# A two-layer sandwich on one core: blocks of 32x32 and TensorE in place of transposing transfers

## The chip, the cores and the metric

The kernel runs on one core of one Trainium2 chip. The metric is the device time of one execution in microseconds (us), here the median of three runs. One further execution was recorded by the hardware profiler, and every row below is of that one.

The names of the engines are those of the profile: PE is TensorE (PEld its weight loads), DVE is VectorE, ACT is ScalarE, POOL is GpSimd, and SP is SyncE, which here does nothing but wait on semaphores and issue transfers.

## The reference

The input is 4096 tokens of width 512. An attention layer with 16 heads works on 64 fixed latent keys instead of on other tokens, and a ternary feed-forward layer follows. Each is wrapped in a layernorm before and one behind:

```python
Q, V = ln(x) @ Wq.T + bq, ln(x) @ Wv.T + bv
logits = einsum('bhtd,lhd->bhtl', Q, latent) / sqrt(HD)
topk_logits, idx = top_k(logits, 4)              # 4 of the 64 latents
weighted = softmax(topk_logits) @ latent[idx]
x1 = x + ln((weighted + V) @ Wo.T + bo)
wu, wg, wd = (clip(round(w / mean(|w|)), -1, 1) * mean(|w|) for w in (W_up, W_gate, W_down))
hidden = silu(ln(x1) @ wu.T) * (ln(x1) @ wg.T)   # 2048 wide
out = x1 + ln(hidden @ wd.T)
```

## The kernel before, in words

The tokens go through in eight chunks of 512, each of four tiles of 128 tokens. The instruction streams of the five engines are written out by hand and are tied together by semaphores; nothing reorders them. A loop body carries the attention of chunk i together with the feed-forward network (FFN) of chunk i-1. The body `first` has the attention of chunk 0 and all the preparation of the weights, `mid` is a hardware loop over chunks 1 to 6, `last` has the attention of chunk 7, and `tail` only the FFN of chunk 7.

**Precision.** Each f32 operand is split into two fp16 halves, high and low. The high half is a rounded copy on ACT, the low half a subtraction on POOL or DVE. A projection is then three products (hi·hi, hi·lo, lo·hi) on PE.

**Layouts.** PE contracts over partitions, so the normalised rows X of a tile, the top-4 probabilities P and the normalised rows X1 ahead of the FFN must all be turned from token-major to feature-major. Before, SP issues a DMA_TRANSPOSE for each tile: `pt` (L363, P into PT), `transpose_rows` (L313, X into XT and X1 into X1T). Weights arrive as they are and are turned on PE (L449 in f32; L472 in fp16 for the ternary weights).

**One period of the loop.** PE does the FFN's `upgate(e)` for e = 0 to 15 into the four banks `ug` (L562), with the logits (L507) in between, then the value projections v(0) to v(3) (L480), `weigh` (L532, which needs PT of all four tiles), the output projection wo (L545), the down products `down(t)` (L574) between them, and the query projections of the next chunk. Behind the upgates ACT takes tanh, DVE multiplies (L1228, L1233), ACT makes the high half (L818) and POOL the low half `hidden_lo` (L985). The attention of tile t runs beside it: eight maxima for each head on DVE (L1243), the replacing of the top four (L1265), `shift` on POOL (L972), the exponential on ACT, `normalise` on POOL (L979), and `probs_lo` on DVE (L1285).

## Time and profile before

| what | value |
|---|---|
| median of three runs | 1121.09 us (1120.2 to 1122.27) |
| profiled execution, its own time | 1121.47 us |
| its span in the trace | 1119.5 us |
| mean granted clock of PE over the span | 0.955 |
| PE busy | 995.2 us, 89% |
| DVE / POOL / ACT busy | 68% / 48% / 46% |

The span runs from the first to the last instruction that the profiler recorded. The execution's own time is 2.0 us longer. The shares are averages over the whole span, and the first 194 us look very different from the rest; the rows below are picked by stage for that reason.

### The profile page before, as it was taken

The page shows a single profiled execution, that of the slowest core. Times are in us where ns is not written, and L with a number is a line of the kernel's source. Part 1 is how long each engine was busy: PE and PEld are TensorE (multiplying, and loading weights), DVE is VectorE, ACT ScalarE, POOL GpSimd, SP SyncE. Part 2 cuts the span into 40 slices and gives each one's busy share as a digit, 9 for nine tenths or more (in the row PEclk, how much of TensorE's full clock was granted, in tenths as well). Part 3 has the DMA queues.
Part 4 walks back from the last instruction along what each step waited for, and adds up shares of the span by engine and source line. Part 5 has one row for each costly group of instructions (what it writes and reads, how often), then busy time and mean ns, then how long its engine had stood idle before and what let it go on. Part 6 is the DMA issues. An engine that isn't in the chain of part 4 may idle for free.

```text
span 1119.5 us, 18366 instructions
## 1 busy us (share of the span) xinstructions
PE 995.2 (89%) x5876; PEld 492.6 (44%) x5876; DVE 757.5 (68%) x2698; ACT 514.1 (46%) x793; POOL 539.8 (48%) x436
## 2 busy tenths in 40 slices
PE   2533368999999999999999999999999999988997
PEld 1232234544454445444544445444544454434443
DVE  6389666796669846993689477966698469835432
ACT  3368554453455345444455444534553454422331
POOL 1145423365546554665456554655456545632332
PEclk9865599999999999999999999999999999999999
DMA  7921243022421243124402431224212421212001
GB/s 225 357 93 40 39 85 72 24 39 57 95 76 19 50 100 95 19 38 94 104 10 38 94 74 58 38 56 94 76 19 41 109 48 20 39 38 57 1 1 38
DMA packets 152451, 74.65 MB, mean 67 GB/s; under 512 B 136768, under 2 KB 136768, under 8 KB 151360
## 3 DMA queue, kind: packets, MB, share of 16 engines
q1 hardware_dynamic: 152384, 73.95, 26.9%
q8 instruction: 19, 0.31, 0.1%
q14 instruction: 48, 0.39, 0.1%
HBM read 31.99 MB, written 8.39 MB: 36 GB/s over the span
## 4 chain that ended last, share of the span: by engine, by line
PE 58%; DVE 17%; issue 10%; ACT 6%; POOL 5%; DMA 3%; SPq 1%; POOLq 0%; DVEq 0%; ACTq 0%
PE ug L562 35%; PE ug L574 11%; PE ring L480 6%; PE ring L545 3%; PE ring L507 2%; DVE Lr L1265 1%; DMA X1T<-halves 1%; POOL halves L1008 1%; DVE stx L1356 1%; DVE x L1353 1%; DVE halves L1285 1%; DVE row L1333 1%; POOL qaT_lo L966 1%; DVE halves L1223 1%; DVE sty L1336 1%
## 5 line engine op out<-in xcount | busy, mean ns | idle before, releaser
L562 PE MATMUL ug<-X1T,TU 128*128 128x512 f16 (+1 forms) x1152 | 247.3, 358 | 11.9 <-DMA X1T<-halves 6.2
L985 POOL TENSOR_TENSOR hT<-ugt,hT 128x512 f16<-128x512 f32 x128 | 168.9, 1320 | 162.0 <-ACT hT L818 162.0
L562 PE MATMUL ug<-X1T,TG 128*128 128x512 f16 (+1 forms) x1152 | 246.4, 357 | 0.0
L574 PE MATMUL ug<-TD,hT 128*128 128x512 f16 x1024 | 225.0, 379 | 0.0
L811 ACT ACTIVATE ugt<-ug,cu 128x512 f32<-128x512 f32 x128 | 88.0, 687 | 237.1 <-PE ug L562 236.1
L562 PEld LDWEIGHTS ug<-X1T,TU 128*128 128x128 f16 x1152 | 111.5, 99 | 121.8 <-issue 7.2
L1228 DVE SCALAR_TENSOR_TENSOR ugt<-ugt,ug 128x512 f32<-128x512 f32 x128 | 87.4, 683 | 112.8 <-ACT ugt L811 111.3
L562 PEld LDWEIGHTS ug<-X1T,TG 128*128 128x128 f16 x1152 | 113.5, 99 | 109.5
L574 PEld LDWEIGHTS ug<-TD,hT 128*128 128x128 f16 x1024 | 99.8, 98 | 122.7 <-issue 3.9
L1265 DVE MATCH_REPLACE8 Lr<-v,Lb 128x68 f32<-128x68 f32 x512 | 102.3, 211 | 0.0
L1292 DVE BATCH_NORM_STATS2 stf<-ug 128x6 f32<-128x512 f32 x32 | 22.2, 693 | 111.9 <-PE ug L574 111.9
L1233 DVE SCALAR_TENSOR_TENSOR ugt<-ugt,ug 128x512 f32<-128x512 f32 x128 | 87.9, 687 | 4.4
L480 PE MATMUL ring<-XT,wq_hi 128*128 128x512 f16 x256 | 78.0, 387 | 12.9 <-DMA XT<-PT 12.9
L972 POOL TENSOR_TENSOR Lb<-Lb,v 128x1024 f32<-128x1024 f32 x32 | 63.5, 1983 | 53.3 <-DVE Lr L1265 46.4
L979 POOL TENSOR_TENSOR p<-Lb,r 128x1024 f32<-128x1024 f32 x32 | 63.8, 1995 | 48.6 <-issue 38.4
L818 ACT ACTIVATE hT<-ugt 128x512 f16<-128x512 f32 x128 | 79.5, 621 | 2.6 <-DVE ugt L1233 2.6
L480 PE MATMUL ring<-XT,wv_hi 128*128 128x512 f16 x256 | 78.3, 388 | 0.0
L1243 DVE MAX8 v<-Lb 128x8 f32<-128x64 f32 x512 | 69.0, 208 | 7.6 <-ACT Lb L766 7.6
L786 ACT ACTIVATE halves<-p 128x1024 f16<-128x1024 f32 x32 | 33.5, 1047 | 52.0 <-POOL p L979 42.6
L1285 DVE SCALAR_TENSOR_TENSOR halves<-p,halves 128x1024 f16<-128x1024 f32 x32 | 52.8, 1651 | 0.0
L680 ACT ACTIVATE xn<-x,nbx,rsx 128x512 f32<-128x512 f32 x28 | 22.7, 811 | 63.6 <-DVE nbx L1367 43.7
L545 PE MATMUL ring<-wo_hi,qaT_hi 128*128 128x512 f16 x128 | 48.5, 379 | 2.6 <-POOL qaT_lo L966 2.6
(172 smaller groups left out, 1490.6 us busy)
## 6 DMA issues: line engine op xcount, KB each, us to landing
x_in<-in_L_attn_hidden_states SPq DMA_DIRECT2D x8, 1024.0 KB, 5.7
out_dram<-Lr SPq DMA_DIRECT2D x32, 256.0 KB, 3.2
x<-in_L_attn_hidden_states SPq DMA_DIRECT2D x28, 256.0 KB, 3.3
hT<-in_L_ffn_W_up SPq DMA_DIRECT2D x8, 512.0 KB, 7.7
hT<-in_L_ffn_W_down SPq DMA_DIRECT2D x8, 512.0 KB, 4.2
TD<-in_L_ffn_W_gate SPq DMA_DIRECT2D x4, 512.0 KB, 11.7
TU<-in_L_attn_Wq SPq DMA_DIRECT2D x1, 1024.0 KB, 7.8
TG<-in_L_attn_Wv SPq DMA_DIRECT2D x1, 1024.0 KB, 9.4
```

What stands on the lines that cost most here:

```text
L480: last = pe.matmul(ring[:, bank, :], wT[w][a][:, k, m * P:(m + 1) * P], XT[:, b, k, :], start=(n == 1), stop=(stop and n == 3 * KD), skip_ ...
L545: last = pe.matmul(ring[:, bank, :], qaT[a][:, k, t * P:(t + 1) * P], wT[2][b][:, k, :], start=(n == 1), stop=(n == 3 * KD))
L562: last = pe.matmul(ug[:, 2 * (e % 2) + s, cols], w[:, k, e * P:(e + 1) * P], X1T[:, b, k, cols], start=(k == 0 and b == 0), stop=(k == KD ...
L574: last = pe.matmul(ug[:, t, :], hT[:, a, e, t * P:(t + 1) * P], td[:, e, :], start=(e == 0 and a == 0), stop=(e == NE - 1 and a == 1))
L811: act.activation(ugt[:, e % 2, :], ug[:, 2 * (e % 2), :], ACT.Tanh, scale=cu[:, 0:1]).then_inc(tanh_ready, 1)
L818: act.activation(hT[:, 0, e, :], ugt[:, 2 + e % 2, :], ACT.Copy).then_inc(h_hi, 1)
L985: pool.tensor_tensor(hT[:, 1, e, :], ugt[:, 2 + e % 2, :], hT[:, 0, e, :], ALU.subtract).then_inc(h_lo, 1)
L1228: dve.scalar_tensor_tensor(out=ugt[:, e % 2, :], in0=ugt[:, e % 2, :], scalar=1.0, in1=ug[:, 2 * (e % 2), :], op0=ALU.add, op1=ALU.mult).t ...
L1233: dve.scalar_tensor_tensor(out=ugt[:, 2 + e % 2, :], in0=ugt[:, e % 2, :], scalar=HS, in1=ug[:, 2 * (e % 2) + 1, :], op0=ALU.mult, op1=ALU ...
L1243: last = dve.max(v8[:, t % 2, h, :], Lb[:, t % 2, h, 0:NL])
L1265: last = dve.match_replace(Lr[:, h, :], v8[:, t % 2, h, :], Lb[:, t % 2, h, :], HIT)
L1285: dve.scalar_tensor_tensor(out=halves[:, 1, :], in0=Pb, scalar=PS, in1=halves[:, 0, :], op0=ALU.mult, op1=ALU.subtract).then_inc(p_lo, 1)
```

## The change

It does four things.

1. No transfer transposes. X1 goes through PE: `turn_x1` does eight transposes of each tile into a bank of PSUM, and a copy on ACT (three tiles of a chunk) or DVE (one) brings it to X1T. P and X are turned on DVE in blocks of 32x32, and plain transfers then move the blocks between partitions: 16 for each tile of P (L469), and two times 16 for a chunk's X (L481). PT and XT are laid out in blocks of 32 columns for it.
2. The host lays out Wq, Wv, Wo, the latents and the FFN's weights transposed. PE's transposes of weights and their evictions are gone. A ternary piece is now a rounding in place on DVE (`round_to`, 24 of them) and a sign on ACT.
3. On POOL a `warm` partition_all_reduce on a zeroed tile stands at the very start, all_maxima(0) comes between the low halves of tile 0 and tile 1, and the low halves of P of tiles 0 to 2 are made on POOL (for tile 2 behind `normalise(3)`), with DVE keeping tile 3.
4. A new body `second` is split from the loop for chunk 1. It carries 14 of the roundings beside its FFN, with the signs that follow them and with all_sum(2) on POOL in the middle. The order of PE in the loop becomes v0 v1 down0 v2 v3 down1 weigh down2 wo down3, and in the tail the last statistics close on DVE.

```diff
-            def transpose_rows(dst, t, src, done):
-                sp.dma_start_transpose(dst[:, :, :, t * P:(t + 1) * P].rearrange("p s k t -> p (s k) t"),
...
-                    sp.dma_start_transpose(PT[:, :, :, t * P:(t + 1) * P].rearrange("p s k t -> p (s k) t"),
-                                           halves[:, :, :].rearrange("p s d -> p (s d)")).then_inc(p_t, 16)
+                    src = prob_halves(kind, t).rearrange("p u s d -> p u (s d)")
+                    for a in range(4):
+                        for u in range(4):
+                            sp.dma_start(PT[BLK * u:BLK * u + BLK, 4 * t + a, :, :, :].rearrange("p s j t -> p (s j t)"),
+                                         src[BLK * a:BLK * a + BLK, u, :]).then_inc(p_t[t % 2], 16)
...
+                def turn(bank, half, done):
+                    for b in range(8):
+                        last = pe.transpose(bank[:, b * P:(b + 1) * P], half[:, b * P:(b + 1) * P], id16[:, :])
+                    last.then_inc(done, 1)
...
+            pool.memset(warm[:, :], 0.0).then_inc(consts, 1)
+            pool.partition_all_reduce(warm[:, 1:2], warm[:, 0:1], P, RMAX).then_inc(warmed, 1)
...
+            def round_to(n):
+                w, src = n // NPIECE, (again_d if n >= 2 * NPIECE else stages[n // NPIECE])[n % NPIECE]
+                dve.tensor_scalar(src, src, iw[:, w:w + 1], MAGIC, ALU.mult, ALU.add).then_inc(rounded, 1)
...
+                def turn(t):
+                    wait(dve, p_raw, i, TT, t + 1)
+                    wait(dve, p_lo, i, TT, t)
+                    dve.transpose(turned[:, :, :].rearrange("p u (j l) -> p u j l", l=BLK),
+                                  Pb.rearrange("p (j u l) -> p u j l", u=4, l=BLK)).then_inc(p_turned, 1)
```

**POOL at the start.** In the order of the built programs, POOL began like this before; `rs` is the first layernorm's reciprocal root, `ma` the maxima, `tota` a sum, and `qaT_lo` a low half of Q.

```order
L930 TENSOR_TENSOR rs<-va,nh 128x4 [waits ln1_var,consts]
L940 ISA
L940 ISA ma<-mg 128x2 [waits mg_ready]
L946 ISA tota<-tot 128x1 [waits tot_ready]
L962 ISA
L962 TENSOR_TENSOR qaT_lo<-p,qaT_hi 128x512 [waits q_hi] x3
L940 ISA
L940 ISA ma<-mg 128x2 [waits mg_ready]
L962 ISA
L962 TENSOR_TENSOR qaT_lo<-p,qaT_hi 128x512 [waits q_hi]
```

And now, with the low halves of X in `PT`:

```order
L1305 ISA
L1305 ISA warm<-warm 128x1 [waits consts]
L1309 ISA
L1309 TENSOR_TENSOR rs<-va,nh 128x4 [waits ln1_var]
L1326 TENSOR_TENSOR PT<-qaT_hi,PT 128x512 [waits x_hi]
L1317 ISA
L1317 ISA ma<-mg 128x2 [waits mg_ready]
L1326 ISA
L1326 TENSOR_TENSOR PT<-qaT_hi,PT 128x512 [waits x_hi]
L1326 TENSOR_TENSOR PT<-qaT_lo,PT 128x512 [waits x_hi] x2
L1342 TENSOR_TENSOR qaT_lo<-p,qaT_hi 128x256 [waits x_lo,qa_hi]
```

A reduction with its two reconfigurations now stands ahead of `rs`, and another behind the first low half. Over the whole program there are 12 reconfigurations where there were 8.

**SP in the loop.** SP's rows for the probabilities before, one transfer for a tile, with the REGISTER_ALU rows between them left to the waits:

```order
L229 REGISTER_ALU
L363 DMA_TRANSPOSE PT<-halves 128x16x128 [waits p_lo,vw_done]
L229 REGISTER_ALU
L363 DMA_TRANSPOSE PT<-halves 128x16x128 [waits p_lo,vw_done] x2
L229 ISA
```

And now, for the last two tiles and what stands behind them:

```order
L256 REGISTER_ALU
L469 DMA PT<-halves 32x512 [waits p_lo,vw_done]
L469 DMA PT<-halves 32x512 x15
L469 DMA PT<-halves 32x512 [waits p_lo,vw_done]
L469 DMA PT<-halves 32x512 x15
L256 ISA
L486 ISA [waits out_ready]
```

Each tile's one instruction has become sixteen in SP's queue, 64 for a chunk, and the store of the output and the transfers of X stand behind them.

**POOL at the end of the loop's FFN.** Before, `hT` being the FFN's hidden values and `Lb` and `p` the logits and probabilities:

```order
L972 TENSOR_TENSOR Lb<-Lb,v 128x16x64 [waits replaced]
L229 REGISTER_ALU
L985 TENSOR_TENSOR hT<-ugt,hT 128x512 [waits h_hi]
L229 REGISTER_ALU
L930 TENSOR_TENSOR rs<-va,nh 128x4 [waits ln1_var]
L979 TENSOR_TENSOR p<-Lb,r 128x1024 [waits p_lo,p_raw,recip_ready]
```

And now:

```order
L1372 TENSOR_TENSOR p<-Lb,v 128x1024 [waits p_turned]
L256 REGISTER_ALU
L1383 TENSOR_TENSOR hT<-ugt,hT 128x512 [waits h_hi]
L1377 TENSOR_TENSOR p<-p,r 128x1024 [waits e_ready,recip_ready]
L1357 TENSOR_TENSOR halves<-turned,halves 128x4x256 [waits p_hi]
L256 REGISTER_ALU
L1309 TENSOR_TENSOR rs<-va,nh 128x4 [waits ln1_var]
```

The normalising of tile 3 has moved ahead of the reciprocal root, and the low half of tile 2 (`halves`, L1357) has come in between.

## Rows read from the trace of the kernel before

**Rows 1.** The page: span and busy time of each engine
```profile
span 1119.5 us, 18366 instructions
...
PE 995.2 (89%) x5876; PEld 492.6 (44%) x5876; DVE 757.5 (68%) x2698; ACT 514.1 (46%) x793; POOL 539.8 (48%) x436
```

**Rows 2.** Windows: start:end, length, busy PE, PEld, DVE, ACT, POOL, clock, DMA share, GB/s
```profile
0.00:194.00 194.00, 87.54 (x612) 53.59 (x612) 131.94 (x390) 106.54 (x157) 63.65 (x50) 0.77 0.45 128
194.20:251.50 57.30, 57.24 (x352) 28.53 (x353) 47.53 (x212) 27.97 (x46) 28.52 (x20) 0.96 0.16 42
434.00:553.00 119.00, 119.00 (x707) 57.85 (x706) 86.11 (x324) 56.48 (x89) 66.02 (x54) 1.00 0.27 62
```

**Rows 3.** Timeline of TensorE in a middle period: start, length, instruction
```profile
489.97 0.59 PE L480 MATMUL ring<-XT,wv_hi 128*128 128x512 f16 x2
...
514.24 0.62 PE L532 MATMUL ring<-PT,latV_hi 64*32 64x512 f16 x16
```

**Rows 4.** Chain that ended last, in the first body: start, length, what
```profile
13.22 3.27 issue
...
33.20 1.15 ACT ug L725 x2
...
48.19 7.57 issue
56.20 7.41 issue
...
130.10 5.79 issue
...
191.05 3.08 DMA X1T<-halves
```

**Rows 5.** Timeline of GpSimd in the first body
```profile
9.16 1.03 POOL L930 TENSOR_TENSOR rs<-va,nh 128x4 f32<-128x4 f32 x1 [6.34 <-DVE va L1177]
16.49 0.37 POOL L940 PARTITION_ALL_REDUCE ma<-mg  x1 [6.31 <-issue]
```

**Rows 6.** Groups of VectorE: line, shapes, count, busy us, mean ns, idle before
```profile
L1285 DVE SCALAR_TENSOR_TENSOR halves<-p,halves 128x1024 f16<-128x1024 f32 x32 | 52.8, 1651 | 0.0
...
L1280 DVE SCALAR_TENSOR_TENSOR Lb<-Lr,Lb 128x1024 f32<-128x1024 f32 x32 | 39.3, 1230 | 0.0
...
L1137 DVE TENSOR_SCALAR ugt<-hT,nhw 128x1024 f16<-128x1024 f32 x8 | 6.0, 746 | 0.0
```

**Rows 7.** Timeline of TensorE: eight fp16 transposes and the next product
```profile
142.01 0.62 PE L472 MATMUL ug<-id,ugt 128*128 128x128 f16 x8 [2.50 <-DVE ugt L1144]
142.47 0.59 PE L480 MATMUL ring<-XT,wv_hi 128*128 128x512 f16 x2
```

**Rows 8.** Timeline of GpSimd at the end of a first FFN stage
```profile
496.23 2.14 POOL L985 TENSOR_TENSOR hT<-ugt,hT 128x512 f16<-128x512 f32 x1
...
502.45 1.90 POOL L979 TENSOR_TENSOR p<-Lb,r 128x1024 f32<-128x1024 f32 x1
```

**Rows 9.** Timeline of SyncE's queue: three reloads issued back to back
```profile
142.98 1.39 SPq L398 DMA_DIRECT2D x<-in_L_attn_hidden_states  x3
```

**Rows 10.** Timeline of SyncE in a middle period: one reload alone
```profile
510.83 0.34 SPq L377 DMA_DIRECT2D x<-in_L_attn_hidden_states  x1
```

**Rows 11.** Timeline of SyncE at the start: four loads of 512 KB
```profile
3.55 2.59 SPq L309 DMA_DIRECT2D hT<-in_L_ffn_W_up  x4
```

**Rows 12.** DMA issues: transfers, KB each, median us from issue to landing
```profile
x<-in_L_attn_hidden_states SPq DMA_DIRECT2D x28, 256.0 KB, 3.3
```

**Rows 13.** The chain that ended last, its part in the tail
```profile
967.08 5.18 PE ring L480 x24
...
982.86 4.26 DMA PT<-halves
...
1028.52 5.17 PE ug L562 x32
...
1112.09 0.71 DVE stf L1292
```

More of the change, by code:

```diff
@@ L49 @@
 TINY = 2.0 ** -100
+NPIECE = 8
+MAGIC = 1.5 * 2.0 ** 23
+HT = CH // 2
+BLK = 32
+PMOVES = 16 * 16
+ON_PE = ()
+MOVED = tuple(t for t in range(TT) if t not in ON_PE)
+LATL = KD * 2 * NL
+LATV = H // 2 * HD
+SMALL = LATL + LATV + 2 * KD
 def ring_jobs(kind):
@@ L70, in ring_plan, with build @@
     at = len(before)
-    return {job: (n % 4, seq[n + at - 4] if n + at >= 4 else None) for n, job in enumerate(jobs)}
-def build(nc, x, Wq, bq, Wv, bv, Wo, bo, lat, Wu, Wg, Wd, out):
+    plan = {job: (n % 4, seq[n + at - 4] if n + at >= 4 else None) for n, job in enumerate(jobs)}
+    if kind == "first":
+        for t in range(TT):
+            plan["WO", 0, t] = (2 + t % 2, ("WO", 0, t - 2) if t >= 2 else None)
+    if kind == "second":
+        for job in (("Q", 0, 0), ("T", -1, 0)):
+            plan[job] = (plan[job][0], None)
+    if kind == "last":
+        for t, bank, freed in ((0, 2, ("WO", 0, 2)), (1, 3, ("WO", 0, 3)), (2, 1, ("WO", 0, 1)), (3, 2, ("T", 0, 0))):
+            plan["T", 0, t] = (bank, freed)
+    return plan
+def build(nc, x, Wq, Wv, Wo, small, bo, Wu, Wg, Wd, out):
     NCH = x.shape[0] * x.shape[1] // CH
@@ new lines, in wide, with down_bank, x_bank @@
+        def wide(v, rows):
+            return v.rearrange("p (a l) -> p a l", l=NL) if len(rows.shape) == 3 else v
+        def down_bank(kind, t):
+            if kind == "last" and t == TT - 1:
+                return ring[:, plans["last"]["WO", 0, 0][0], :]
+            return ug[:, t, :]
+        def x_bank(kind, c, t):
+            if kind == "first" and c == 0:
+                bank = ug[:, t, :]
+            elif kind == "first" and t < 2:
+                bank = ring[:, t, :]
+            else:
+                bank = ug[:, t % 2, :]
+            return bank.bitcast(F16)
@@ L412, in body @@
                 if ffn and nxt:
                     reload(2)
+                if ffn:
                     out(2)
[L415 to L420 removed]
                     out(3)
@@ new lines, in body @@
+                    x0_lo(0)
+                    all_maxima(0)
+                    x0_lo(1)
+                    x0_lo(2)
+                    x0_lo(3)
+                    for m in range(KD):
+                        low_q_half(m, 0)
+                    all_maxima(1)
+                    for m in range(KD):
+                        low_q_half(m, 1)
+                    shift(0)
+                    normalise(0)
+                    shift(1)
+                    probs_lo(0)
+                    normalise(1)
@@ new lines, in body @@
+                    probs_lo(1)
+                    shift(2)
+                    all_sum(0)
+                    normalise(2)
+                    for m in range(KD):
+                        low_a_half(m, 0)
+                    shift(3)
+                    probs_lo(2)
+                    ln1_rstd_of(1)
+                    normalise(3)
+                    rstd_y(0)
+                    probs_lo(3)
+                    rstd_y(1)
+                    rstd_x(0, 0)
+                    rstd_x(0, 1)
@@ new lines, in body @@
+                    for m in range(KD):
+                        low_a_half(m, 1)
+                    all_sum(1)
+                    s1_lo(1, 0)
+                    s1_lo(1, 1)
+                    s1_lo(1, 2)
+                    s1_lo(1, 3)
+                    rstd_y(2)
+                    rstd_y(3)
+                    rstd_x(0, 2)
+                    rstd_x(0, 3)
+                    return
+                for m in range(KD if att else 0):
+                    low_q(m)
+                late = kind == "second"
```

1381 lines of the change are left out of this document (894 added, 487 removed).

## The prediction, made blind

> **What bounds the kernel now.** I read the page first: PE is busy 995.2 us of the span of 1119.5 [rows 1]. An average over stages says little, so the windows come next. In a middle period PE works 119.00 of 119.00 us at full clock, while DVE has 86.11 and POOL 66.02 [rows 2]: the loop is bounded by TensorE's own work. The value products v(0) of chunk i start every 119.28 us, from (967.08 - 489.97) / 4 [rows 3, 13], so under 0.4 us of a period is idle. In the first 194 us PE works 87.54 and its mean clock is 0.77 [rows 2]. There nothing is full: DVE 131.94, ACT 106.54, POOL 63.65. What sets that stretch is a chain, and the chain that ended last shows pieces called "issue" of 3.27, 7.57, 7.41 and 5.79 us [rows 4]. On POOL they lie around the partition_all_reduce: the first has 6.31 us idle ahead of it with no releaser, though rs ahead of it ended at 10.19 and the maxima came only at 13.2 (the issue piece starts at 13.22) [rows 4, 5]. I read this as the change of POOL's code, which starts as soon as the instruction before it is done and takes 6 to 7.5 us in each direction, while the reduction itself takes 0.37 [rows 5]. A rule of the Trainium skill stands beside this (GPSIMD Engine Reference, Instruction dispatch): the first call of a freshly loaded kernel pays about 6 us; the trace agrees, and shows that the way back pays it as well.
>
> The changed kernel thus has three places to win or lose: the first body, the body of chunk 1, and the loop, where anything added to PE or waited for by PE is paid in full six times.
>
> **First body: about 14.5 us earlier.** It is a chain through POOL. Warm starts at about 2 us and costs a change each way, 6.3 + 0.4 + 6.8, which ends rs near 18 where it ran at 9.16 [rows 5]. The low half of tile 0 follows at 21, then all_maxima(0) with its two changes, 13.5 us, to 34. Three low halves, the scaled weights and eight half-width query products take 14 us, to 48. all_maxima(1), with the 7.57 and 7.41 of the row and 0.4 between them [rows 4], ends at 63.6, just where it did before. Then ACT has 22 absolute sums; two took 1.15 a piece in the chain with their reading out [rows 4], about 27 us, and with the exponentials between them I take 32, to 96. all_sum(0) on POOL takes 93.4 to 106.4, the attention of tiles 2 and 3 and its low halves reach 136, all_sum(1) with two changes 149.2, the low halves of chunk 1's rows and a pair of copies 164.2, and four query products with the turns of X1 178.7. Before, the same point was at 194.26 less the roughly 1.1 us that the first upgates lost to half clock behind the wait for X1T [rows 4]: 193.2. The gain is 14.5. Of the 48 f32 and 192 fp16 transposes of weights that vanish from PE nothing counts, since PE was busy under half of this stretch [rows 2]. Bounds: with all ten changes hidden (the five pairs are 68.6 us, of which ACT's sums would still keep about 6) it would be 116; with all ten at 7.8, the longest of the chain's pieces and its start [rows 4], it would be 188.
>
> **The body of chunk 1: about 12.7 us later.** From the first upgate to v(0) it took 57.3, with DVE busy 47.53 [rows 2]. DVE now gets 14 roundings at 0.746 [rows 6] = 10.4, three block transposes of 1024 columns, and a copy of X1 of about 1.1; it gives two low halves of 1.65 to POOL [rows 6]. No row has a block transpose: I take 1.23, the row of the 1024-wide f32 select beside it, in bounds of 0.75 and 2.1 (one and near three passes) [rows 6]. That is 47.5 + 10.4 + 3.7 + 1.1 + 0.7 of small ones - 3.3 = 60.1 of work. It had 9.8 us of idle there; I leave it 5.9 of that, so that the stage takes 66. On top, all_sum(2) holds POOL for two changes: the low half of hidden 7 comes some 13 us late, the `ug` banks are not freed, and upgate(11) waits. I take 5.5 of the 7.6 that this comes to, since part coincides with DVE's lag: 71.5, so 58.8 + 12.7. Bounds: 58.8 if all of it fits, 77.8 with no idle saved and the full wait. v(0) of chunk 1 then starts at 178.7 + 71.5 = 250.2, against 251.5 [rows 2].
>
> **The loop: 4.5 us more in each period.**
> - *Transposes on PE.* Eight of them delay the next product by 142.47 - 142.01 = 0.46 us [rows 7]. Four tiles: +1.84, wholly on PE and without cover. The 0.35 of idle may absorb some: I subtract it.
> - *DVE at the head of the loop.* Two rounds of maxima now come ahead of hidden(0), so upgate(2) waits for its bank: +0.9 (bounds 0 and 2.1).
> - *The wait of weigh.* PE needed PT 514.24 - 489.97 = 24.3 us after v(0) [rows 3]. The low half of hidden 15 ended on POOL 8.4 after v(0) because shift(3) stood ahead of it [rows 8]; shift(3) is now earlier, so I put normalise(3) (1.90 [rows 8]) and the low half of tile 2 behind it at 11.1 (bound 9.2). From there SP must issue 32 transfers one behind another. The three reloads of 1.39 give a pitch of (1.39 - 0.43) / 2 = 0.48 [rows 9]; one alone takes 0.34 [rows 10]; at the start it is 2.59 / 4 = 0.65 [rows 11]. Mine have 32 partitions, not 128: I take 0.42. The last lands 2.2 behind its issue, below the 3.3 of 256 KB [rows 12]. So 11.1 + 31 x 0.42 + 2.2 = 26.3, and PE waits 26.3 - 24.3 = 2.0, say 2.1 with the semaphore. Behind weigh stand down(2), wo and the whole second half of the period on PE, so nothing hides it. Ends: 9.2 + 31 x 0.34 + 1.5 = 21.2 gives no wait; 11.1 + 31 x 0.48 + 3.3 = 29.3 gives 5.0; at 0.65 it is 10.
>
> Together 1.84 - 0.35 + 0.9 + 2.1 = 4.5: a period of 123.75. X's 32 transfers land about 48 us behind v(0) and are needed at 52, so they cost nothing while the pitch stays below 0.55. The period from chunk 1 to 2 lacks the first body's idle and comes to 122.3. ACT's three copies of X1 in a period (1.0 us each) lie beside 56 us of work in 119 [rows 2] and are hidden.
>
> A rule of the Trainium skill speaks against this part (DMA: Bandwidth & Descriptors, Rules for kernel authors): many small transfers should be coalesced, since below 64 KB one pays mostly overhead. Each of these has 32 KB. In this trace the share of the DMA engines is only 0.27 [rows 2], so what it would cost here is the queue's pitch, which is the term above.
>
> **The tail.** weigh of the last chunk waited 4.26 for a transposing transfer [rows 13]; that wait becomes one for 16 plain ones, about 1.1 later. The first upgates of the tail are released about 3 us earlier, since a bank no longer waits for the statistics ahead of 1028.52 [rows 13], but PE is behind by the reordering of down(3). The close on DVE instead of POOL saves 1.5 behind 1112.09 [rows 13]. Together 152.0 where it was 152.4.
>
> **Sum.** 250.2 + 122.3 + 5 x 123.75 + 152.0 = 1143.3 of span. Before, the profiled run took 2.0 more than its span and lay 0.4 above the median, so the median comes to 1144.
>
> **The rivals.**
> - *A. As worked out*, 1144, in its own range of 1136 to 1154: chance 0.44.
> - *B. SP's queue is slower than I take it.* The ground for it is the start, where four issues took 2.59 [rows 11]; against it, the 0.48 of rows 9. At 0.6 weigh waits 7.7 instead of 2.1: 5.6 in each of six periods, so 1144 + 34 = 1178; at 0.5 it is 1158. With it goes the dearer block transpose (2.1 instead of 1.23), which makes DVE late for P by 3.5 in a period of which perhaps 1.5 to 1.8 reaches PE: 1144 + 10 = 1154. Chance 0.18, from 1154 up. A page of the Trainium skill (VectorE: DVE Perf Modes, The three transpose paths) gives 311 ns for 128x128 in bf16; by eight times that my 1024 columns would take 2.5 us, and the time would be the 1154 named here. No row here shows one.
> - *C. POOL's changes of code mostly lie under other work* (the other side). The switch ahead of a reduction begins before its data is ready, as it did at 10.19; if the data is always late, only the ways back cost, and warm costs nothing at all. Then the first body ends at about 150 instead of 178.7, chunk 1's v(0) at 221.5, and the time is 1144 - 28.7 = 1115; with PE also free of a wait in the loop (-12.6) 1103, and with no cost of the changes at all 1080. It decides from the point where v(0) of chunk 1 starts before 226: the loop and the tail give back 6 x 4.5 - 2 = 25, which is what the start must win. For it: DVE and ACT had 62 and 87 us of idle in the first 194 [rows 2]. Against: the chain passes through four of the waits already. Chance 0.25.
> - *D. Between them*, 1119 to 1136: SP's pitch is 0.37 and PE never waits for PT (1144 - 12.6 = 1131), or the roundings fit into chunk 1's FFN (1144 - 12.7 = 1131), or both. Chance 0.13, with 0.04 of it within 0.2% (2.2 us) of before, which is what a measurement of this kernel can tell from no change.
>
> The range of 1106 to 1168 leaves out the far ends of B and C, about 0.1 each. Faster 0.25, same 0.05, slower 0.70.
>
> **What would show it.** In the changed trace: rs on POOL at about 18 instead of 9; 11 to 15 us around each reduction; the first upgate of chunk 1's body near 179; v(0) of chunk 1 near 250, and DVE over 90% busy in the 70 us ahead of it; v(0) to v(0) of 123.75 in the loop; PE idle by about 2 us ahead of weigh with a DMA of PT as the releaser; 0.46 us for eight transposes. I am wrong above all if the start of v(0) of chunk 1 lies before 226 or if weigh waits over 5 us.

## The result, and the profile after

The changed kernel takes 1254.9 us (median of four runs, 1252.5 to 1256.0) against 1121.7 of the kernel before, measured beside it: a ratio of 1.118, with an interval of 1.116 to 1.121. It is 133 us slower. The prediction said slower, at 1144, and its range ended at 1168.

The page of the changed kernel, with its span, its busy times and the granted clock in 40 slices, answers to [rows 1]:

```profile
span 1250.6 us, 19370 instructions
...
PE 1023.4 (82%) x6112; PEld 500.5 (40%) x6112; DVE 778.9 (62%) x2740; ACT 551.2 (44%) x843; POOL 553.8 (44%) x469
...
PEclk9966769879889989998999989998999899998999
```

PE has 28 us more of busy time and 131 us more of span: most of the loss is waiting. The windows answer to [rows 2]; they are the first body, the FFN beside chunk 1's attention, the rest of that body up to v(0) of chunk 2, and one period of the loop:

```profile
0.00:192.80 192.80, 73.21 (x584) 43.12 (x585) 92.85 (x341) 98.81 (x157) 60.36 (x63) 0.77 0.28 107
192.80:277.20 84.40, 67.18 (x394) 32.28 (x393) 55.70 (x226) 48.73 (x71) 34.13 (x24) 0.88 0.08 25
277.20:421.30 144.10, 125.28 (x737) 60.18 (x736) 98.91 (x342) 63.77 (x98) 70.15 (x57) 0.93 0.19 53
689.70:823.40 133.70, 123.77 (x738) 59.88 (x736) 92.68 (x335) 59.40 (x91) 68.49 (x56) 0.96 0.17 48
```

The forecast had the first upgate at 178.7 (it came at 192.8), v(0) of chunk 1 at 250.2 (277.2), v(0) of chunk 2 at 372.5 (421.3), periods of 123.75 (133.9 on average) and a tail of 152.0 (1250.6 - 1090.7 = 159.9). The miss of 107.3 us of span is thus 14.1 in the first body, 12.9 in the FFN of chunk 1, 21.8 in the rest of that body, 50.6 in five periods, and 7.9 in the tail. Of the two signs of being wrong that the prediction named, one came true: weigh waits over 5 us.

One point of the kernel before has to be set right. The prediction takes 194.2 for the start of chunk 1's body [rows 2], but TensorE's timeline of the kernel before has the first upgate earlier:

```profile
185.93 1.04 PE L562 MATMUL ug<-X1T,TU 128*128 128x256 f16 x8
...
194.26 1.87 PE L562 MATMUL ug<-X1T,TU 128*128 128x256 f16 x8 [4.67 <-DMA X1T<-halves]
```

At 194.26 it only goes on, behind a wait. So the first body before took 185.9 us and the FFN beside chunk 1's attention 65.7, not 57.3. The first body has become 6.9 us longer, and that FFN 18.7.

**One period of the loop.** SP's timeline of the changed kernel, which answers to [rows 9 to 11]; "x64" rows merge issues whose first starts at the first column and whose last ends that many us later:

```profile
662.66 58.16 SPq L469 DMA_DIRECT2D PT<-halves  x64
...
722.36 10.27 SPq L481 DMA_DIRECT2D XT<-xh  x16
...
738.06 10.20 SPq L481 DMA_DIRECT2D XT<-xh  x16
748.59 0.34 SPq L495 DMA_DIRECT2D x<-in_x  x1
```

GpSimd's timeline at the end of the FFN, for [rows 8]:

```profile
696.45 1.90 POOL L1377 TENSOR_TENSOR p<-p,r 128x1024 f32<-128x1024 f32 x1 [1.07 <-DVE r L1709]
698.30 2.13 POOL L1357 TENSOR_TENSOR halves<-turned,halves 128x1024 f16<-128x1024 f32 x1
```

v(0) of this period began at 689.7. The low half of tile 2 ends at 700.4, 10.7 behind it (11.1 forecast). From there 32 issues fill SP up to 720.8: 0.64 us each, not 0.42. Sixteen issues for X take 10.27, again 0.64. TensorE's timeline shows what waits, for [rows 3, 7]:

```profile
722.19 1.05 PE L723 MATMUL ring<-PT,latV_hi 64*32 64x512 f16 x16 [8.13 <-DMA PT<-halves]
...
724.88 8.13 PE L782 MATMUL ug<-TD,hT 128*128 128x512 f16 x32
...
750.12 0.59 PE L582 MATMUL ring<-XT,wq_hi 128*128 128x512 f16 x2
...
752.71 0.61 PE L589 MATMUL ring<-id,xh 128*128 128x128 f16 x8
...
759.31 0.61 PE L589 MATMUL ring<-id,xh 128*128 128x128 f16 x8 [0.37 <-DVE xh L1654]
...
762.34 1.04 PE L765 MATMUL ug<-X1T,TU 128*128 128x256 f16 x8
```

The same places in the timeline of the kernel before, whose v(0) is at 489.97 [rows 3]:

```profile
515.66 7.08 PE L574 MATMUL ug<-TD,hT 128*128 128x512 f16 x32
...
539.84 0.59 PE L480 MATMUL ring<-XT,wq_hi 128*128 128x512 f16 x2
...
550.20 1.04 PE L562 MATMUL ug<-X1T,TU 128*128 128x256 f16 x8
```

weigh starts 32.5 behind v(0), after 8.13 us of idle that a transfer of PT ended, where it started 24.3 behind [rows 3]. The down product behind it takes 8.13 where it took 7.08; that its time equals the idle's is chance. The four turns of X1 are the L589 rows, of which one waits 0.37 for the last tile. Two windows show the clock behind the wait, and the FFN:

```profile
722.20:732.80 10.60, 10.60 (x80) 4.31 (x81) 0.00 (x0) 5.05 (x8) 4.62 (x4) 0.77 0.32 87
762.30:823.40 61.10, 59.66 (x394) 30.89 (x392) 51.77 (x215) 31.78 (x52) 36.21 (x26) 1.00 0.14 42
```

In the 10.6 us from weigh on the mean granted clock is 0.77: TensorE runs part of them at 1.2 GHz, after 8 us of idle. So the 14.4 us that a period gained split like this: 8.2 up to weigh, 2.3 from weigh to q(0), the first query product (the clock), 1.9 from q(0) to the first upgate (three turns of 0.46 and the wait), and 2.0 in the FFN (the fourth turn and two waits of 0.7). The landing itself is quicker than I took it, as the page's rows of transfers say:

```profile
PT<-halves SPq DMA_DIRECT2D x448, 32.0 KB, 1.8
...
XT<-xh SPq DMA_DIRECT2D x192, 32.0 KB, 1.9
```

**The first body.** GpSimd's timeline, for [rows 5]. The idle in brackets ahead of a reduction is the change of code towards it, that of the row behind it the change back:

```profile
10.45 0.38 POOL L1305 PARTITION_ALL_REDUCE warm<-warm  x1 [8.67 <-issue]
21.33 1.05 POOL L1309 TENSOR_TENSOR rs<-va,nh 128x4 f32<-128x4 f32 x1 [10.50 <-issue]
...
31.17 0.37 POOL L1317 PARTITION_ALL_REDUCE ma<-mg  x1 [5.85 <-issue]
38.56 1.14 POOL L1326 TENSOR_TENSOR PT<-qaT_hi,PT 128x512 f16<-128x512 f32 x1 [7.02 <-issue]
...
61.33 0.37 POOL L1317 PARTITION_ALL_REDUCE ma<-mg  x1 [9.90 <-issue]
73.42 1.29 POOL L1342 TENSOR_TENSOR qaT_lo<-p,qaT_hi 128x256 f16<-128x256 f32 x2 [11.72 <-issue]
...
111.93 0.40 POOL L1321 PARTITION_ALL_REDUCE tota<-tot  x1 [5.80 <-issue]
119.33 1.89 POOL L1377 TENSOR_TENSOR p<-p,r 128x1024 f32<-128x1024 f32 x1 [6.99 <-issue]
```

The changes cost 8.67 and 10.50 us around warm, 5.85 and 7.02 around the first maxima, 9.90 and 11.72 around the second, 5.80 and 6.99 around the first sum. I had 6.3 to 7.6 for all. What differs between them is the traffic, seen in windows over four of these gaps (the last two columns are the share of the DMA engines and GB/s):

```profile
10.90:21.30 10.40, 0.00 (x0) 0.00 (x0) 0.00 (x0) 0.00 (x0) 0.00 (x0) 1.00 0.99 406
25.60:31.20 5.60, 0.88 (x8) 0.61 (x6) 0.00 (x0) 3.43 (x5) 0.03 (x1) 1.00 0.00 0
61.80:73.40 11.60, 0.00 (x0) 0.00 (x0) 1.01 (x8) 0.00 (x0) 0.00 (x0) 0.50 0.77 288
112.40:119.30 6.90, 0.00 (x0) 0.00 (x0) 0.00 (x0) 0.00 (x0) 0.00 (x0) 0.50 0.00 0
```

Where the DMA engines are idle a change costs 5.8 to 7.0; where they are busy, 8.7 to 11.7. The share alone does not give the size. In the kernel before, two changes towards a reduction met busy DMA engines too, in these windows:

```profile
10.20:16.40 6.20, 3.24 (x17) 2.72 (x15) 3.12 (x7) 5.45 (x8) 0.00 (x0) 1.00 0.79 295
48.00:55.70 7.70, 1.76 (x34) 1.50 (x29) 0.00 (x0) 0.00 (x0) 0.00 (x0) 0.50 0.88 348
```

They took 6.31 [rows 5] and 7.80.

### The profile page after: what moved, and what is told of

It reads as the page before. It is cut to its first block, busy times and chain, and to the rows that moved or that the text cites. A ratio compares the mean times of both kernels' runs of the same rounds, so it can differ in the third digit from the quotient of the medians.

```text
span 1250.6 us, 19370 instructions
## 1 busy us (share of the span) xinstructions
PE 1023.4 (82%) x6112; PEld 500.5 (40%) x6112; DVE 778.9 (62%) x2740; ACT 551.2 (44%) x843; POOL 553.8 (44%) x469
## 4 chain that ended last, share of the span: by engine, by line
issue 26%; POOL 20%; SPq 18%; PE 16%; DVE 11%; ACT 6%; DMA 2%; POOLq 0%; DVEq 0%; ACTq 0%
SPq L469 10%; PE ug L765 8%; SPq L481 8%; POOL hT L1383 6%; PE ug L782 4%; POOL p L1377 4%; POOL p L1372 3%; POOL halves L1357 3%; PE ring L582 2%; DMA x<-in_x 1%; PE ring L744 1%; DVE Lr L1696 1%; DVE ugt L1659 1%; DVE v L1674 1%; POOL qaT_lo L1333 1%
## 5 line engine op out<-in xcount | busy, mean ns | idle before, releaser
L765 PE MATMUL ug<-X1T,TU 128*128 128x512 f16 (+1 forms) x1152 | 249.9, 361 | 22.2 <-DVE ugt L1664 20.3
L1383 POOL TENSOR_TENSOR hT<-ugt,hT 128x512 f16<-128x512 f32 x128 | 148.8, 1162 | 211.7 <-ACT hT L1116 204.4
L582 PE MATMUL ring<-XT,wq_hi 128*128 128x512 f16 (+1 forms) x288 | 80.7, 368 | 9.3 <-DMA XT<-xh 7.4
L1740 DVE STREAM_TRANSPOSE turned<-xn 128x512 f32<-128x512 f32 x24 | 17.1, 711 | 113.6 <-ACT xn L882 113.0
L1372 POOL TENSOR_TENSOR p<-Lb,v 128x1024 f32<-128x1024 f32 x30 | 58.9, 1963 | 27.1 <-DVE v L1674 26.5
L582 PE MATMUL ring<-XT,wv_hi 128*128 128x512 f16 x224 | 66.6, 379 | 0.0
L1377 POOL TENSOR_TENSOR p<-p,r 128x1024 f32<-128x1024 f32 x30 | 57.0, 1900 | 19.2 <-DVE r L1709 8.8
L723 PE MATMUL ring<-PT,latV_hi 64*32 64x512 f16 x224 | 15.1, 623 | 60.5 <-DMA PT<-halves 60.5
L1361 POOL TENSOR_TENSOR qaT_lo<-p,qaT_hi 128x512 f16<-128x512 f32 x28 | 32.4, 1156 | 61.8 <-ACT qaT_hi L1091 60.7
L1051 ACT ACTIVATE halves<-turned 128x1024 f16<-128x1024 f32 x28 | 29.5, 1053 | 54.7 <-DVE turned L1730 54.7
## 6 DMA issues: line engine op xcount, KB each, us to landing
hT<-in_Wu SPq DMA_DIRECT2D x4, 512.0 KB, 10.7
```

Source lines behind the costliest of these rows:

```text
L582: last = pe.matmul(bank, wT[w][a][:, k, m * P:(m + 1) * P], XT[:, cols, b, k, :], start=(n == 1), stop=(stop and n == 3 * KD), skip_group_ ...
L765: last = pe.matmul(ug[:, 2 * (e % 2) + s, cols], w[:, k, e * P:(e + 1) * P], X1T[:, b, k, cols], start=(k == 0 and b == 0), stop=(k == KD ...
L1372: pool.tensor_tensor(prob_buf(kind, t), Lb[:, t % 2, :, 0:NL], v8[:, t % 2, :, 0:1].broadcast_to([P, H, NL]), ALU.subtract).then_inc(shift ...
L1377: pool.tensor_tensor(prob_buf(kind, t), prob_buf(kind, t), r4[:, t % 2, :].rearrange("p (h a) -> p h a", a=1).broadcast_to([P, H, NL]), AL ...
L1383: pool.tensor_tensor(hT[:, 1, e, :], ugt[:, 2 + e % 2, :], hT[:, 0, e, :], ALU.subtract).then_inc(h_lo, 1)
```

## The experiments

Where an experiment leaves work out, its expectation says which. Each ratio is to the kernel before, measured beside it, whose medians lay between 1118.0 and 1121.7. A period is the mean distance of v(0) from chunk 3 on; where X's transfers are late, the first one in the loop is 1 to 2 us longer.

### e1: one transfer for a tile

```diff
-PMOVES = 16 * 16
+PMOVES = 16
...
-                            sp.dma_start(PT[BLK * u:BLK * u + BLK, 4 * t + a, :, :, :].rearrange("p s j t -> p (s j t)"),
-                                         src[BLK * a:BLK * a + BLK, u, :]).then_inc(p_t[t % 2], 16)
+                    sp.dma_start(PT[:, 4 * t:4 * t + 4, :, :, :].rearrange("p a s j t -> p a (s j t)"), src).then_inc(p_t[t % 2], 16)
...
+                    sp.dma_start(xt_runs[:, 8 * n:8 * n + 8, :],
+                                 xh[:, :, :].rearrange("p t (u d) -> p (t u) d", u=4)).then_inc(x_landed[n], 16)
```

> The changed kernel, in which each tile of P goes in one transfer of 128 partitions (128 KB) and each pair of tiles of X in one of 256 KB, instead of 16 each. Left out: the exchange between groups of 32 partitions, so every byte of PT and XT is still written, but with rows in the wrong group. Theory 1 (SP's queue): a plain transfer of 32 partitions takes 0.64 us of SP's queue however small it is, 32 of them stand between the low half of tile 2 and weigh (20.4 us), 32 more for X hold the reload of x behind them. Without them the wait of 8.1 us ahead of weigh is gone, PE stays at full clock, XT and the reload land in time, and a period of the loop comes to 123 to 125 instead of 133.7; over seven chunks with the tail about -70 us, so 1175 to 1190. Rival (the transposes on PE, the block transposes on DVE and the later order on POOL carry the loss): the period stays above 129 and the time above 1215.

Measured: 1162.0 (ratio 1.038, 1.035 to 1.041), a period of 121.76. SP's timeline of this kernel:

```profile
546.08 0.49 SPq L476 DMA_DIRECT2D XT<-xh  x1
...
617.98 43.26 SPq L467 DMA_DIRECT2D PT<-halves  x4
```

One issue takes 0.49, and four tiles of P are spread over 43 us because each waits only for its data. PE no longer idles ahead of weigh. The queue's theory holds, and with 93 us it is worth more than the 70 I gave it. The rest of chunk 1's body falls from 144.1 to 126.8 and the tail from 159.9 to 150.2. A period keeps 2.5 over before: 1.84 of turns and about 0.7 of waiting for a bank in the FFN. Those were my first two terms of the loop, 2.4 together.

### e2: pairs of tiles

```diff
+                    if t % 2 == 0:
+                        return
...
+                            sp.dma_start(PT[BLK * u:BLK * u + BLK, 8 * n + a:8 * n + a + 5:4, :, :, :].rearrange("p a s j t -> p a (s j t)"),
+                                         src[BLK * a:BLK * a + BLK, :, u, :]).then_inc(p_t[n], 16)
```

> The changed kernel with two tiles of P in one transfer: 16 transfers of 64 KB for a pair, issued when the second tile of the pair is ready, so 32 for a chunk instead of 64; the result is the full one. Theory 1: if an issue costs 0.6 to 0.65 whatever it carries, the last pair takes 16 x 0.64 = 10 us from the low half of tile 3 (about 13 us behind v(0)), lands near 25.5, and weigh waits 1 us or less: -7 to -9 us in each of seven chunks, with the clock's share -50 to -75, so 1180 to 1205. If the issue's cost grows with the bytes or descriptors (1.2 us for 64 KB), nothing is won: 1250 within 10. The rival of the DVE and PE chain: 1235 or more.

Measured: 1219.0 (1.089, 1.086 to 1.092), a period of 128.5. It is complete, and 36 us faster than the changed kernel, which is less than expected. The issues did not get dearer with twice the bytes:

```profile
668.63 10.24 SPq L471 DMA_DIRECT2D PT<-halves  x16
```

Sixteen of 64 KB take 10.24 us, 0.64 each. But the last pair, which waits for the low half of tile 3, is issued from 15.7 us behind v(0) on and not from the 13 I assumed, and weigh still waits 3.3 us.

### e3 and e4: no warm, and no reduction at all

```diff
-            pool.partition_all_reduce(warm[:, 1:2], warm[:, 0:1], P, RMAX).then_inc(warmed, 1)
```

and for e4 also

```diff
-                pool.partition_all_reduce(tota[:, w:w + 1], tot[:, w:w + 1], P, RADD).then_inc(tota_ready, 1)
+                pool.tensor_tensor(tota[:, w:w + 1], tot[:, w:w + 1], tot[:, w:w + 1], ALU.add).then_inc(tota_ready, 1)
...
```

The maxima are replaced in the same way, and the factor behind the sums is 64 times as large.

> The changed kernel without the reduction on a zeroed tile at the very start. Theory 2 (POOL's changes of code set the first body): rs ran at 21.3 because warm and its two changes of code take it from 1.8 to 21.3; without them rs runs at 9 to 10, and the first body ends 8 to 12 us earlier: -8 to -12 in all. Rival a (ACT and DVE set it from 60 us on): the chain catches up by the waits for all_maxima(1), under 3 us. Rival b (warm does what its name says, the later changes are cheap only because of it): the first change behind it gets dearer by 5 us or more and the time is within 3 us of before or worse.

> The changed kernel without any partition_all_reduce: the two maxima and three sums on POOL are an ordinary addition of the same columns with itself, so that scales are those of a partition and not of the matrix, which is the part left out, and warm is left out too. Every wait stays. Theory 2: the six reductions with twelve changes of code hold POOL 19.5 + 13.2 + 22 + 13.2 + 13.8 us in the first body, and 13 in the next; with all gone the first upgate comes 45 to 60 us earlier than 192.8 (the rest is bounded by ACT's sums), and the FFN of chunk 1 loses 5 to 10 of its 84 us: -50 to -70 in all, 1180 to 1200. Rival (loads, ACT and DVE bound the first body): under -20.

Measured: e3 1244.8 (1.113, 1.109 to 1.116), e4 1188.0 (1.061, 1.058 to 1.065). In e3 the first upgate comes at 181.8 instead of 192.8, so warm's price passes through the whole first body. GpSimd's timeline of e3:

```profile
20.78 0.37 POOL L1316 PARTITION_ALL_REDUCE ma<-mg  x1 [8.10 <-issue]
...
50.43 0.37 POOL L1316 PARTITION_ALL_REDUCE ma<-mg  x1 [9.50 <-issue]
62.84 1.29 POOL L1341 TENSOR_TENSOR qaT_lo<-p,qaT_hi 128x256 f16<-128x256 f32 x2 [12.05 <-issue]
```

The first maxima stand 10.4 us earlier than in the changed kernel. The change towards them is 2.3 us dearer than with warm (8.10 against 5.85, now beside the loads) and not 5 or more, and the time falls by 10, so rival b falls. In e4 the first upgate comes at 134.6, 58 us earlier, and v(0) of chunk 1 at 210.5, 67 earlier: the first body is a chain through POOL's changes of code, as the prediction took it. What a reduction costs is mostly not the reduction (0.4 us).

### e5: sixteen wide transfers

```diff
-                            sp.dma_start(PT[BLK * u:BLK * u + BLK, 4 * t + a, :, :, :].rearrange("p s j t -> p (s j t)"),
-                                         src[BLK * a:BLK * a + BLK, u, :]).then_inc(p_t[t % 2], 16)
+                            sp.dma_start(PT[:, 4 * t + a, :, :, :].rearrange("p s j t -> p (s j t)")[:, P * u:P * u + P],
+                                         src[:, a, P * u:P * u + P]).then_inc(p_t[t % 2], 16)
```

> The changed kernel with 16 transfers for each tile of P as before, but each of 128 partitions by 256 bytes instead of 32 partitions by 1 KB (the same 32 KB). Left out: the exchange between groups of partitions. It tells what the 0.64 us between issues hangs on. If on the number of transfers queued back to back: weigh waits about 8 us as in the changed kernel, time 1250 within 10. If on the partitions or pieces in a transfer: at 0.48 a piece (as one of 128 partitions took alone in the kernel with one move for a tile) the wait falls by 5 and the time to about 1215; if it grows with 128 rows of 256 bytes, it is over 1280.

Measured: 1256.5 (1.122, 1.120 to 1.125), a period of 133.9. SP's timeline, where 64 issues take what they took in the changed kernel (58.16):

```profile
664.58 58.37 SPq L469 DMA_DIRECT2D PT<-halves  x64
```

Neither 128 partitions for 32, nor twice the bytes (e2), changes the pitch: for these transfers from SBUF to SBUF it is paid by the issue. It is not one number for the whole queue. In the changed kernel seven loads of 512 KB were issued back to back between 43.05 and 46.30, one every 0.47 us. What makes the difference was not tried.

### e6: the kernel before without its reductions

```diff
-                pool.partition_all_reduce(ma[:, 2 * g:2 * g + 2], mg[:, 2 * g:2 * g + 2], P, RMAX).then_inc(ma_ready, 1)
+                pool.tensor_tensor(ma[:, 2 * g:2 * g + 2], mg[:, 2 * g:2 * g + 2], mg[:, 2 * g:2 * g + 2], ALU.add).then_inc(ma_ready, 1)
```

The sums are replaced as in e4.

> The kernel before, without its five partition_all_reduces (each an ordinary addition of the same column, so that scales are a partition's own; this is the part left out). Theory 2 says that the start of this kernel too is set by POOL's changes of code: 8 changes, of which 7.2 + 7.6 + 7.4 + 5.8 us and 3.3 stand in its chain as issue. I expect the first upgate 20 to 30 us earlier and the time near 1095. Rival (they lie beside loads and ACT's sums here): within 5 of before.

Measured: 1096.8 (0.979, 0.978 to 0.981); the first upgate comes at 163.2 instead of 185.9, 23 us earlier. The start of the kernel before is held by the same thing.

### e7, e9, e13 and e14: what makes the FFN of chunk 1 long

```diff
+                if n in (3, 11, 6, 14, 20, 21, 16, 7, 15, 17, 18, 19, 22, 23):
+                    src = src[:, 0:2]
                 dve.tensor_scalar(src, src, iw[:, w:w + 1], MAGIC, ALU.mult, ALU.add).then_inc(rounded, 1)
```

This is e7. For e9 and e14, on the same 14 pieces:

```diff
+                    dve.tensor_scalar(matrix(n), source(n), iw[:, w:w + 1], 1.0, ALU.mult, ALU.min).then_inc(rounded, 1)
...
+                        act.activation(matrix(n)[:, 0, 0:2], matrix(n)[:, 0, 0:2], ACT.Copy).then_inc(tern_ready, 1)
```

e13 is e7 with e4's edit, and e14 is e9 with it.

> The changed kernel in which the 14 roundings beside the FFN of chunk 1 work on 2 columns of 1024 (the rest of those weights is left unrounded, which is the part left out); all waits and ACT's signs stay. The FFN of chunk 1 took 84.4 us where 57.3 stood before. If DVE's added work is what it waits for, 14 x 0.7 = 10 us of it go and the stage comes to 73 to 76, the time to 1243. If ACT's signs (17 us of work on the way of the tanh) or the halt of POOL around all_sum(2) carry it: over 80, and 1250.

> The changed kernel, in which the 14 pieces that are made ternary beside the FFN of chunk 1 are written by VectorE's one pass (scaled and cut off at 1 from above, not rounded and not cut off from below, which is the part left out), and ScalarE's 14 signs of 1.03 us become copies of 2 columns. DVE's work stays, the thin roundings having moved the stage by 2.6 us only. If the signs in front of the tanh hold it, the FFN of chunk 1 falls from 84.4 us to 70 to 75 and the time to about 1240; if it is the halt of POOL around all_sum(2) alone (9 us), it stays at 82 or more, 1250.

> The changed kernel without partition_all_reduces (scales are a partition's own) and with the 14 late roundings on 2 columns (the rest left unrounded): both parts are left out. Without the reductions alone the FFN of chunk 1 took 75.9 us, before the change 57.3. If VectorE's roundings were hidden behind the halt of POOL, now 7 to 10 us go: 66 to 69, and the time 1180. If it is the order or ScalarE: 73 or more, 1187.

> The changed kernel without partition_all_reduces and with the 14 late signs of ScalarE as copies of 2 columns, VectorE writing the pieces in one pass of the same length as the rounding (not rounded, not cut off from below: left out). If ScalarE's 14.4 us of signs stand in front of the tanh, the FFN of chunk 1 falls from 75.9 to 64 to 68; if VectorE's work or the order carries it, 72 or more.

Measured, as times and as length of the stage from the first upgate to v(0) of chunk 1:

| kernel | time | stage |
|---|---|---|
| before | 1121.7 | 65.7 |
| changed | 1254.9 | 84.4 |
| e7, thin roundings | 1251.8 | 81.8 |
| e9, no signs | 1248.2 | 82.1 |
| e4, no reductions | 1188.0 | 75.9 |
| e13, both of e4 and e7 | 1184.6 | 72.9 |
| e14, both of e4 and e9 | 1178.8 | 70.4 |

The expectations set 57.3 beside this stage, which is the count from 194.2; from the first upgate on it is 65.7. e7 and e9 came out where one part alone does not carry the stage (81.8 is over 80, 82.1 is over 82). e13 and e14 fell between their two cases. In no run did the roundings or the signs alone carry the stage. In the changed kernel's stage TensorE's longest idle is the halt of POOL around all_sum(2), in its timeline the row

```profile
251.15 3.60 PE L765 MATMUL ug<-X1T,TU 128*128 128x512 f16 x8 [9.07 <-DVE ugt L1664]
```

and the reductions account for 8.5 us of the stage. With them gone the roundings are worth 3.0 and the signs 5.5. The signs are worth as much again behind the stage: up to v(0) of chunk 2 e9 needs 140.6 us where the changed kernel needs 144.1. A period's FFN in the loop takes 61.1, so of the 23.3 that the stage has over it, 17 are accounted for if these add. The remaining 6 (the absolute sums on ScalarE, the later logits, the order on VectorE) were not taken apart and stay open.

### e8, e10 and e12: the last tile through TensorE, P alone in one move, and the sum of two gains

```diff
-ON_PE = ()
+ON_PE = (3,)
...
                     v(2)
                     v(3)
+                    turn_p(3)
                     down(1)
```

e10 is e1's edit on P alone, and e12 is e8 with e3's edit. Code cuts of e8 leave out the waits and the two copies on ACT.

> The changed kernel with the last tile of P turned on TensorE (16 transposes into two free banks, between v(3) and down(1), and two copies on ACT) in place of its block transpose and 16 transfers; the result is the full one. By the queue theory the last transfers are those of tile 2: 10.7 + 10.2 + 1.8 = 22.7 behind v(0), ahead of weigh's 24.3, so the wait of 8.1 and the half clock behind it go, at 0.9 of transposes and 2 at most of waiting for the copies: a period of 124 to 127, a time of 1185 to 1205. If what weighs is the work on PE, it gets slower than 1255.

> The changed kernel with one transfer of 128 partitions for each tile of P (left out: the exchange between groups), and X's 2 x 16 transfers as they are. With both in one move a period was 121.76, with neither 133.68. By the queue theory the wait ahead of weigh (8.1, and the half clock behind it) is P's alone, while X's 32 issues (20.5 us of SP) hold the last reload of x: I expect 123 to 125 a period, 1170 to 1185. If X's share is larger (the reload late by 5 or more), 127 or more.

> The changed kernel, complete, with the last tile of P through TensorE (1193.4) and without the reduction on a zeroed tile at the start (-9 by itself). One lies in the loop, the other in the first body, so they should add: 1182 to 1187. The rest against before (1119) is then the other two tiles' and X's transfers and POOL's remaining ten changes of code.

Measured: e8 1193.4 (1.067, 1.065 to 1.068), a period of 124.7; e10 1187.8 (1.061, 1.059 to 1.063), a period of 123.9; e12 1186.3 (1.060, 1.058 to 1.061). e10's period is as expected, its time 3 us above the range. e8 is complete and wins 61 us by taking 16 of 96 issues away from the place where they are waited for. In its period TensorE has one new idle, ahead of the 16 transposes, for the bank of down(0), which ACT reads out behind its statistics:

```profile
559.94 1.05 PE L615 MATMUL ug<-id,halves 128*128 128x128 f16 x16 [1.46 <-ACT Lr L1126]
```

Between e10 and e1 lies X's share: 2.1 us a period. P's is 9.8. This is so in that order; in the changed kernel itself the two stretches behind q(0) are about 1.4 us longer than in e1. e12 wins 7 us over e8, where the same edit won 10 over the changed kernel, and lies in its range.

### e15: the loads held back

```diff
-            sp.wait_ge(x_turned, TT)
+            sp.wait_ge(q_lo, 1)
             load_ffn(2, Wd, 0, 1)
```

> The changed kernel, complete, with SP holding the 19 later loads of FFN weights until the second maxima are done and POOL is back at the low halves of Q (a later start of the loads, so the time itself will rise, by up to 15 us). The two changes of code around the second maxima took 9.9 and 11.7 us with the DMA engines at 100 and 77%. If the DMA traffic makes them dear, they fall to 5.5 to 7.5 each, and the first two around warm stay as they are; if it is the kind or the place, they stay above 9.

(There are 15 such loads.) Measured: 1245.6 in a single run, beside 1118.0 of before. GpSimd's timeline of this kernel:

```profile
9.70 0.38 POOL L1305 PARTITION_ALL_REDUCE warm<-warm  x1 [7.92 <-issue]
19.52 1.05 POOL L1309 TENSOR_TENSOR rs<-va,nh 128x4 f32<-128x4 f32 x1 [9.45 <-issue]
...
56.27 0.37 POOL L1317 PARTITION_ALL_REDUCE ma<-mg  x1 [5.78 <-issue]
63.74 1.29 POOL L1342 TENSOR_TENSOR qaT_lo<-p,qaT_hi 128x256 f16<-128x256 f32 x2 [7.10 <-issue]
```

The changes around the second maxima fall from 9.90 and 11.72 to 5.78 and 7.10, and those around warm, whose loads were left alone, stay at 7.9 and 9.5. Around the second maxima the seven other versions that keep warm and all reductions (e1, e2, e5, e7 to e10) have 9.3 to 10.4 and 11.4 to 12.9. So the traffic makes them dear; by what way is not shown. The later loads cost nothing that shows: the first upgate comes at 182.8 instead of 192.8, and the time did not rise but fell, as far as one run can say.

### e11: the kernel before with its reductions on TensorE

The one complete version that beats both. The maxima of two columns are laid on a diagonal and multiplied by a matrix of ones, so that every partition gets all 128 values, and VectorE takes the maximum over the row; a sum is one product of ones with its column.

```diff
+                def spread(g):
+                    pe.wait_ge(mg_ready, g + 1)
+                    pe.matmul(ug[:, 2, 0:2 * P], ones[:, :], dg[:, :, :].rearrange("p c k -> p (c k)"),
+                              start=True, stop=True).then_inc(red_done, 1)
...
+                def total(w):
+                    pe.wait_ge(tot_ready, w + 1)
+                    pe.matmul(ug[:, 2, 2 * P + w:2 * P + w + 1], ones[:, :], tot[:, w:w + 1],
+                              start=True, stop=True).then_inc(tota_ready, 1)
```

> The kernel before, complete, with its five reductions over partitions taken off POOL: the two maxima go as a diagonal matrix against a matrix of ones through TensorE in f32 and a maximum over the row on VectorE, the three sums as one product of ones with the column. No change of POOL's code is left. With the reductions simply left out it was 1096.8 against 1119.2; TensorE and VectorE get about 2 us for each maximum and 0.5 for each sum: I expect 1098 to 1104, faster than both kernels. If TensorE's or VectorE's queue behind the new waits holds the start, 1110 or more.

Measured: 1104.4, a ratio of 0.987 (0.985 to 0.989) to the kernel before, and complete. TensorE's timeline of its start:

```profile
14.89 0.67 PE L467 MATMUL ug<-dg,ones 128*128 128x256 f32 x2 [0.80 <-DVE dg L1135]
...
37.04 0.28 PE L472 MATMUL ug<-tot,ones 128*128 128x1 f32 x2
```

A product of 0.3 to 0.7 us, with VectorE's part of the maxima beside it, has taken the place of 9 to 16 us of POOL. Of e6's 22 us it keeps 15; the first upgate comes at 168.1 instead of e6's 163.2. What makes that difference was not tried.

## Why the prediction was wrong

The direction was right and the sum was not: 107 us of span short. About three quarters of it lie in one term, the transfers: e1 takes 93 us away, where the sum held 6 x 2.1 + 1.1 = 13.7 for them. By its own steps:

- **The pitch of SP's queue** ("I take 0.42") is the term that failed first. It is 0.64 for any of these transfers (e2, e5). The start's 2.59 / 4 = 0.65 [rows 11] would have been right, and neither the reload alone (0.34) nor the three together (0.48) [rows 9, 10]. But no row had a plain transfer from SBUF to SBUF, loads of 512 KB have come at 0.47 as well, and so 0.65 would have been right by luck. The prediction prices a pitch of 0.65 at 10 us of wait a period, and its range ends far below that. The reason I gave for going low, fewer partitions, is what e5 shows to be without effect. With 0.64 the formula of the prediction gives 11.1 + 31 x 0.64 + 1.8 = 32.7 for weigh, and it was 32.5: the mechanism was right and the size was off.
- **What follows from the wait** was not in the sum, nor in rival B: 2.3 us a period of half clock behind it. Nor did X's transfers stay hidden. They landed 60 us behind v(0) and not 48, at the very moment of q(0), with the last reload behind them: 2.1 us where P's wait is gone (e10 against e1), 1.4 where it is not. B's 1178 for a pitch of 0.6 was thus too low even by itself. Moved transfers are also paid most where the queue is fullest: the rest of chunk 1's body waited 11.7 for PT and 6.4 for XT. Of its 21.8 over the forecast, 17.3 go with e1. The tail's 7.9 are the same wait, 8.16 ahead of its weigh.
- **The turns on TensorE** at 0.46 for eight and **the head of the loop** (0.9) were right, the second roughly (0.7): with no wait for transfers a period is 121.76 (e1), where these terms give 121.7.
- **The block transpose** was taken at 1.23 and takes 1.245:

```profile
L1730 DVE STREAM_TRANSPOSE turned<-p 128x1024 f32<-128x1024 f32 x28 | 34.9, 1245 | 1.0
```

  A page of the Trainium skill (VectorE: DVE Perf Modes, The three transpose paths) gives 311 ns for 128 columns in bf16, from which the 2.5 us of rival B was estimated. The measurement decides: half of that.
- **The first body** had its mechanism right (e3, e4, e6) and its prices low. Of the 14.1, 12.7 lie in the four changes of code that met busy DMA engines: 8.67 + 10.50 + 9.90 + 11.72 against the 28.1 taken. The bound took 7.8 for the longest change. The kernel before has a longer one, of which its chain shows 7.17, and which the rows do not have:

```profile
44.14 2.26 POOL L962 TENSOR_TENSOR qaT_lo<-p,qaT_hi 128x512 f16<-128x512 f32 x2 [9.10 <-issue]
```

  The rule of the Trainium skill (GPSIMD Engine Reference, Instruction dispatch), about 6 us for the first call, agrees where the DMA engines are idle (5.80 to 5.95 towards a reduction in the changed kernel) and not where they are busy (8.67 and 9.90). The gain of 14.5 was besides counted from the wrong point of the kernel before: the forecast's own 178.7 was 7.2 ahead of the first upgate at 185.93, and the body came out 6.9 behind it.
- **The FFN of chunk 1** was put down to VectorE's load, over 90% busy. That step was wrong: VectorE was busy 55.70 of the 84.40 us, 66%, and three of the 14 roundings and the third block transpose came only behind v(0). The roundings were worth 2.6 (e7), the halt of POOL 8.5 where I gave it 5.5, and the signs on ScalarE, which had no term, 5.5 (e14 against e4). The base was wrong too: it counts from 194.2 and so leaves out 8.4 us of the stage, up to that much of the 12.9 missing. Six us over a period's FFN stay open.
- **Rival C**, the one for faster, had the right idea in the wrong kernel: without the changes of code the start wins 67 us (e4) and the changed kernel would still be at 1188, since against the kernel before the bodies behind v(0) of chunk 1 lose 105 us.

The rule of the same skill that many small transfers should be coalesced (DMA: Bandwidth & Descriptors, Rules for kernel authors) points the right way, and e1 bears it out; but the cost here sits in the issuing queue, not in the DMA engines, whose share even fell from 0.27 [rows 2] to 0.17.

## What to carry to other kernels

Count the issues between the last result and its consumer, and multiply by the queue's pitch back to back (0.64 us here): a transfer of 32 KB cost the queue as much as one of 64 KB, and TensorE's wait of 8 us cost 2.3 us of clock as well. Whether a second engine's queue would have halved the wait was not tried. Price a term by the row that is alike in place (issues in a burst, changes of code under load), not by the one that is alike in size. An operation of 0.4 us that needs other code on its engine can cost 13 to 22; look for the idle without a releaser around it, and whether another engine can do it. And when two kernels are set side by side, take the same instruction as the start of a stage in both.

## What the runs showed of the hardware

- An issue of a plain transfer from SBUF to SBUF on SP's queue took 0.60 us with a pitch of 0.64 when many stood behind one another, for 32 partitions by 1 KB, 128 by 256 bytes, or 64 KB in all; one alone took 0.49, a reload from HBM alone 0.34, and seven loads of 512 KB back to back 0.47 each.
- The change of GpSimd's code took 5.8 to 7.4 us with idle DMA engines and 8.7 to 11.7 with busy ones in the changed kernel (7.4 to 12.9 over its versions, and 6.3 and 7.8 in two places of the kernel before), was paid in both directions, and in e15 fell with the traffic at the same place in the program.
- After 8.1 us of idle TensorE's mean granted clock was 0.77 over the next 10.6 us.
- The block transpose on VectorE, f32, took 1.245 us for 1024 columns and 0.711 for 512.
